# A graph and mixture-of-experts layer on Trainium2: experts add straight into the output, and ScalarE multiplies all chunks of the early edge batches

## What is computed

```python
edge_index = jnp.stack([src, dst])                    # 50000 edges, 3125 nodes, sorted by dst
xn = _layernorm(x, axis=-1)                           # x: 3125 x 256
x = x + gnn(xn, edge_index, W, att_src, att_dst, bias) + mix(xn, Wqkv, Wproj, temperature)
x = x + ffn(_layernorm(x, axis=-1), Wg, W1, W2)       # 8 experts, 2 for each token
# gnn: h = x @ W; alpha = softmax over the edges of a node of leaky_relu(a_src[src] + a_dst[dst])
#      out = segment_sum(alpha[:, :, None] * h[src], dst)
# mix: y = sum over second order (pair) features of q against sums over all nodes of k, k, v
# ffn: top-2 gate; out = sum of prob * (relu(x @ W1[e] + b1[e]) @ W2[e] + b2[e])
```

## Time and profile before

| | us |
|---|---|
| median of 3 runs | 1449.74 |
| lowest and highest | 1444.14, 1452.1 |
| the profiled execution, its own time | 1443.35 |
| its span, first to last instruction | 1441.3 |
| PE busy in the span | 1202.2 (83%) |
| DVE / ACT / POOL busy | 847.1 / 609.0 / 669.3 |
| feature steps with edges, and steps 29 to 32 | about 309 to 597 |
| mix stage | about 597 to 912 |
| stores of the attention and mix rows, issued by SP | 929.9 to 960.9 |
| first instruction that waits for these stores (DVE, the slots' one-hots) | 985.7 |
| experts | about 1013 to 1428 |

### The profile page before, as it was taken

How to read it: one execution, slowest core, us unless ns; L and a number is a source line. 1 busy time by engine, 2 the same in 40 slices (tenths; PEclk the granted TensorE clock), 3 DMA queues, 4 the chain that set the end, 5 groups by cost and what they waited for, 6 DMA issues and landing times.

```text
span 1441.3 us, 25299 instructions
## 1 busy us (share of the span) xinstructions
PE 1202.2 (83%) x7992; PEld 865.4 (60%) x7993; DVE 847.1 (59%) x1771; ACT 609.0 (42%) x1967; POOL 669.3 (46%) x626
## 2 busy tenths in 40 slices
PE   3789956748778877899999999275999999999994
PEld 2645533425444544545455556174899999999994
DVE  8599859788888887644545446878222233332221
ACT  1400011444554446587777777250333333333331
POOL 2070000675556556777777777630333333333331
PEclk9999966779988988999999999657999999999997
DMA  5635374432222223333434333773122222222223
GB/s 178 213 121 198 140 283 140 141 94 74 79 83 82 78 80 92 99 114 100 117 114 117 103 115 113 289 277 131 31 36 37 37 36 36 36 36 36 36 36 103
DMA packets 67570, 153.67 MB, mean 107 GB/s; under 512 B 12962, under 2 KB 41559, under 8 KB 66263
## 3 DMA queue, kind: packets, MB, share of 16 engines
q0 software_dynamic: 32640, 75.27, 21.0%
q1 hardware_dynamic: 33478, 74.93, 14.7%
q10 hardware_dynamic: 1360, 2.33, 0.5%
HBM read 131.76 MB, written 23.92 MB: 108 GB/s over the span
## 4 chain that ended last, share of the span: by engine, by line
PE 66%; DVE 20%; issue 4%; DMA 3%; POOL 2%; ACT 1%; DVEq 1%; SPq 0%; POOLq 0%; ACTq 0%
PE ps L1267 15%; PE ps L1560 14%; PE ps L1570 13%; DVE arena L1829 4%; PE ps L1463 4%; PE ps L1208 4%; PE ps L1475 3%; PE ps L1296 2%; PE ps L1217 1%; PE ps L1421 1%; DVEq L1833 1%; PE ps L1175 1%; POOL arena L853 1%; DVE arena L1786 1%; DMA h_d<-arena 1%
## 5 line engine op out<-in xcount | busy, mean ns | idle before, releaser
L853 POOL DMA_INDIRECT arena<-h_d,tables x440 | 449.1, 1021 | 189.5 <-issue 126.1
L1267 PE MATMUL ps<-arena 128*128 128x264 f32 x880 | 246.1, 434 | 86.2 <-DVE acc L1838 63.6
L1267 PEld LDWEIGHTS ps<-arena 128*128 128x128 f32 x880 | 181.2, 214 | 143.9 <-issue 91.4
L970 ACT ACTIVATE arena<-arena 128x64 f32<-128x64 f32 x880 | 222.0, 339 | 17.6 <-DMA arena<-h_d,tables 17.6
L1560 PE MATMUL ps<-acc 128*128 128x128 f32 x1792 | 211.3, 277 | 0.0
L895 POOL DMA_INDIRECT sum_d<-acc,tables x56 | 89.8, 1603 | 254.9 <-DVE acc L2217 247.4
L1560 PEld LDWEIGHTS ps<-acc 128*128 128x128 f32 x1792 | 206.5, 193 | 0.3
L1570 PE MATMUL ps<-arena,acc 128*128 x896 | 202.5, 379 | 0.0
L1137 ACT ACTIVATE acc<-ps,b_s 128x128 f32<-128x128 f32 x448 | 128.1, 369 | 120.1 <-PE ps L1560 120.1
L1570 PEld LDWEIGHTS ps<-arena,acc 128*128 128x128 f32 x896 | 166.0, 190 | 20.3
L2205 DVE COPY acc<-arena 128x1024 f32 x112 | 78.3, 700 | 123.8 <-PE ps L1560 123.3
(11 more groups left out here) (368 smaller groups left out, 1489.6 us busy)
## 6 DMA issues: line engine op xcount, KB each, us to landing
arena<-dl_d SPq DMA_DIRECT2D x22, 640.0 KB, 6.9
arena<-lo_d SPq DMA_DIRECT2D x16, 784.0 KB, 4.4
arena<-h_d,tables POOLq DMA_INDIRECT x440
arena<-in_w SPq DMA_DIRECT2D x4, 1664.0 KB, 11.7
arena<-in_w SPq DMA_DIRECT2D x4, 1632.0 KB, 25.5
arena<-hi_d SPq DMA_DIRECT2D x16, 343.0 KB, 5.1
h_d<-arena SPq DMA_DIRECT2D x25, 128.0 KB, 1.7
sum_d<-res SPq DMA_DIRECT2D x5, 640.0 KB, 7.9
```

Of the source, the lines that this page charges most:

```text
L853: pool.indirect_dma_start(gb[u][:, k, 0:D], None, h_d, bass.IndirectOffsetOnAxis(tsrc[:, j:j + 1], 0)).then_inc(s_gg[u], 16)
L970: ins = A_.activation(v, v, ACT.Copy, scale=wm[:, m + k, h:h + 1])
L1267: last = MM(ps[:, 6 + s, 0:ACOL], oh[b % OB][:, m, :], gb[u][:, m, :], start=(k == 0), stop=(k == TE - 1))
```

## The change

The scratch tensor `sum_d` goes. SP stores the attention and mix rows into `out`, the last tile apart (one DMA more), the experts add into `out`, with a bound on the index so that padding rows are skipped, and the last copy is gone, as is a store of zeros to `sum_d`'s padding rows. Thresholds of `s_zero` and `s_res` follow. In batches below `early` = 50, ACT multiplies all four chunks (16 instructions), DVE's multiply (1853) is left out, and the one-hot instruction raises `s_msg` in its place.

```diff
             for c in range(LC):
                 sp.wait_ge(s_att2, c + 1)
-                sp.dma_start(sum_d[c * LW * P:(c + 1) * LW * P, :].rearrange("(t p) c -> p t c", p=P),
-                             res[:, c * LW:(c + 1) * LW, :]).then_inc(s_res, 16)
+                a, b = c * LW, min((c + 1) * LW, NT - 1)
+                sp.dma_start(ot[:, a:b, :], res[:, a:b, :]).then_inc(s_res, 16)
+                if c == LC - 1:
+                    sp.dma_start(out[(NT - 1) * P:N, :], res[0:TAIL, NT - 1, :]).then_inc(s_res, 16)
...
-            sp.wait_ge(s_fy, 16 * NJ)
-            sp.dma_start(out.rearrange("n c -> (n c)").rearrange("(p w) -> p w", p=P),
-                         sum_d[0:N, :].rearrange("n c -> (n c)").rearrange("(p w) -> p w", p=P)).then_inc(s_res, 16)
             sp.wait_ge(s_res, 16 * (LC + 1))
...
-                pool.indirect_dma_start(sum_d, bass.IndirectOffsetOnAxis(pidx[:, j:j + 1], 0),
-                                        ys[j % 2], None, compute_op=ALU.add).then_inc(s_fy, 16)
+                pool.indirect_dma_start(out, bass.IndirectOffsetOnAxis(pidx[:, j:j + 1], 0),
+                                        ys[j % 2], None, bounds_check=N - 1, oob_is_err=False,
+                                        compute_op=ALU.add).then_inc(s_fy, 16)
...
-                for k in range(KA, SB * TE):
+                for k in range(0 if b < early else KA, SB * TE):
                     for h in range(GH):
                         v = gb[u][:, k, h * GD:(h + 1) * GD]
                         ins = A_.activation(v, v, ACT.Copy, scale=wm[:, m + k, h:h + 1])
...
-                    V.tensor_tensor(oh[b % OB], under(iota_f[:, :], SB * TE), over(tdl[:, m:m + SB * TE], P), ALU.is_equal)
+                    ins = V.tensor_tensor(oh[b % OB], under(iota_f[:, :], SB * TE), over(tdl[:, m:m + SB * TE], P), ALU.is_equal)
+                    if b < early:
+                        ins.then_inc(s_msg, 1)
                     if b >= 2:
                         accumulate(b - 2, 1)
-                    dve.wait_ge(s_gg[u], 16 * SB * TE * (b // NBUF + 1))
-                    v = gb[u][:, 0:KA, 0:D].rearrange("p k (h c) -> p k h c", c=GD)
-                    V.tensor_tensor(v, v, over(wm[:, m:m + KA, 0:GH], GD), ALU.mult).then_inc(s_msg, 1)
+                    if b >= early:
+                        dve.wait_ge(s_gg[u], 16 * SB * TE * (b // NBUF + 1))
+                        v = gb[u][:, 0:KA, 0:D].rearrange("p k (h c) -> p k h c", c=GD)
+                        V.tensor_tensor(v, v, over(wm[:, m:m + KA, 0:GH], GD), ALU.mult).then_inc(s_msg, 1)
```

More of the change, by code:

```diff
@@ L164, in gps_layer @@
         xn_d = dram("xn_d", [NP + P, D])
-        sum_d = dram("sum_d", [NP + P, D])
         AW = 32000
@@ L746, in _ @@
             sp.dma_start(xn_d[NP:NP + P, :], zrow).then_inc(s_zero, 16)
-            sp.dma_start(sum_d[NP:NP + P, :], zrow).then_inc(s_zero, 16)
             sp.wait_ge(s_wl, 1)
@@ L876, in _ @@
                 ins.then_inc(s_own, 1)
-            pool.wait_ge(s_zero, 32)
+            pool.wait_ge(s_zero, 16)
             pool.wait_ge(s_xst, 16 * LC)
@@ L894, in add_results @@
                 pool.wait_ge(s_fw, j + 1)
-                pool.indirect_dma_start(sum_d, bass.IndirectOffsetOnAxis(pidx[:, j:j + 1], 0),
-                                        ys[j % 2], None, compute_op=ALU.add).then_inc(s_fy, 16)
+                pool.indirect_dma_start(out, bass.IndirectOffsetOnAxis(pidx[:, j:j + 1], 0),
+                                        ys[j % 2], None, bounds_check=N - 1, oob_is_err=False,
+                                        compute_op=ALU.add).then_inc(s_fy, 16)
             for j in range(JB - 1):
                 load_tokens(j)
-            pool.wait_ge(s_res, 16 * LC)
+            pool.wait_ge(s_res, 16 * (LC + 1))
             for j in range(NJ):
@@ L1941, in bulk_weights @@
                 dve.wait_ge(s_we, 1)
-                dve.wait_ge(s_zero, 32)
+                dve.wait_ge(s_zero, 16)
                 dve.wait_ge(s_bias, NT)
@@ L2179, in _ @@
             dve.wait_ge(s_xst, 16 * LC)
-            dve.wait_ge(s_res, 16 * LC)
+            dve.wait_ge(s_res, 16 * (LC + 1))
             for k in range(TOPK):
```

## The result

| | before | after |
|---|---|---|
| median, us (20 runs each) | 1449.57 | 1443.81 |
| lowest and highest | 1443.32, 1452.10 | 1441.86, 1447.19 |
| the profiled execution, its span | 1443.35, 1441.3 | 1443.57, 1441.8 |
| last add starts (POOL) | 1424.52 | 1432.42 |
| from there to the end of the span | 16.78 | 9.38 |

The ratio of the runs is 0.997, with a 95% interval of 0.996 to 0.998. The medians lie 5.8 us apart (the ratio makes it 4.3); 13.9 were forecast (1436). Faster was right, the size was not. The profile of before came from one of its fastest executions, that of after from a median one, so the two profiles must not be subtracted as a whole: 7.9 us that after is late at the last add are partly that luck.

A forecast was written before the change was run, and what follows sets the result against it. Bounds: a PE-DVE cycle in feature steps, PE in the mix stage, the uncovered copy at the end. 1443.35 - 12.5 - 1.9 + 0.5 = 1429.5, median 6.4 higher: 1436; range 1426 to 1446.

The forecast's parts named there:

- The copy, -12.5: At the kernel's end: nothing runs beside the copy, so removing it saves 12.5 of the 12.95 us from its issue.
- it doesn't do what it says: Rival at the end: the last add might wait for something else; the prediction saw nothing; no chance listed under this name.
- The adds into `out`, 0 with bounds -2.3 and +3.2: Experts' 56 adds on POOL: a bound check is hidden by 4.4 us idle; 0, between 2.3 sooner and 3.2 later.
- DVE in the steady steps, 0: Feature steps: two DVE multiplies fewer per step only lengthen DVE's idle time by 0.6 us; saved 0.
- ACT's loop, 12.07 against 11.89: Feature steps: ACT's longer loop is hidden in long steps (13.35 us) and 0.18 us over in short ones (11.89).
- 0.5 for the whole stretch: Feature steps from 312 to 534 us: three short steps, lengthened by ACT's loop, cost 0.5 us together.
- PE come to batch 45 0.6 sooner: Before the mix stage: without DVE's multiply of batch 41, PE starts aggregating batch 45 at 589.0, not 589.61.
- The rival in which the clock turns the other way (0.1): Feature steps: three short steps turn long at the low clock, 4.4 us more, giving 1440; chance 0.1, to 1444.
- The entry of the mix stage, 3 us of waits, and the squares 3.4 later: Steps 27 to 32: PE waits for ACT 1.0 and 2.0 us, first squares start at 601.75 instead of 598.38.
- The gathers, -2.2: POOL's gathers between 562 and 598 us: six no longer stretched by DVE's multiplies, last rows land 2.2 us earlier.
- The end of the edge work, -1.9: Where gathers (904.9) meet ACT's last batch (905.2): the later decides, 905.2 for 907.09, saved 1.9 us.
- a slower add: Rival: the bound check or `out` makes adds longer; below 4.4 us each, at most 8.8, 1445; chance 0.08, to 1446.

The follow-up runs named there:

- e6: Output part and no drain, ACT multiplying all four chunks in batches 0 to 37 alone, against the kernel before: ratio 0.9939.
- e7: Output part and no drain, ACT multiplying all four chunks in batches 38 to 49 alone, against the kernel before: ratio 0.9939.
- e12: Output part and no drain, ACT multiplying all four chunks in every second batch of 38 to 49, against the kernel before: 1431.88 us, ratio 0.9909.
- e1: Output part alone (adds into `out` with bound, copy gone, batches shared as before), against the kernel before: 1440.33 us, ratio 0.9967.
- e4: The kernel before without POOL's drain, against the kernel before: 1445.90 us, ratio 0.9996.

## Why the prediction was right, and where it failed

**The copy, -12.5: this step failed. The copy's size was right, what runs beside it was not seen.** "Nothing runs beside the copy" was read from the rows; in the trace of before, 12.5 us of copy hid the 6.3 us of POOL's drain, and taking the cover away exposed it. Between the last add's start and the end 16.78 became 9.38: 7.4 saved, of which 1.1 is the earlier landing, so the copy gave 6.3. This term was 6.2 too large, three quarters of the 8.1 that the sum missed. The prediction's own criterion (the span ends within 1 us of the last add's landing) was the one that failed, and pointed at it. The rival "it doesn't do what it says" said "I see nothing": the question to ask was which engines finish beside the copy, and what each still has to do. The page of the Trainium skill that the prediction sets beside the copy ("DMA: Bandwidth & Descriptors", section "Anatomy of one DMA — SWDGE (gpsimd) path") fits DMAs issued by GpSimd, and this one was issued by SP, so its 9.3 us bear on neither side.

**The adds into `out`, 0 with bounds -2.3 and +3.2: right in sum, as two things cancel that it did not have.** The group of adds, whose answer before is the earlier trace rows:

```profile
L892 POOL DMA_INDIRECT out<-acc,tables x56 | 89.4, 1596 | 255.2 <-DVE acc L2218 247.5 <-issue 5.1 <-DMA out<-acc,tables 2.6
```

1.596 for 1.603, so the add itself costs POOL no more, and the last add, in all kernels with the bound, lands after 2.7 instead of 3.8. That padding rows without a transfer make it shorter was argued, and not measured apart.

Against this gain of 1.1 the slots of the experts run slower. From the start of the 28th add to that of the 50th it is 159.4 us in the three profiles with `sum_d` and 160.6 to 161.1 in the thirteen with adds into `out`. Three slots take 7.5 to 7.7 for 7.1 to 7.3; ahead of the first, POOL's gather of tokens takes longer (the output part alone, then the kernel before), and PE's next products start 4.03 after the ones before them, for 3.67:

```profile
1234.70 1.44 POOL L885 DMA_INDIRECT acc<-xn_d,tables  x1 [0.30 <-issue]
```

```profile
1234.53 0.99 POOL L887 DMA_INDIRECT acc<-xn_d,tables  x1 [0.30 <-issue]
```

From PE's last product of the mix stage (917.87 and 911.06) to the last add it is 514.55 in the changed kernel for 513.46: 1.1 lost. The forecast's "hidden" held for the adds and not for what POOL does between them. Which piece of the output part does it was not tested.

**DVE in the steady steps, 0: right.** No profile shows a step shortened by the missing multiplies; changing the steady batches alone (e6) gained nothing.

**ACT's loop, 12.07 against 11.89: right to 0.01.** The step of 12.08 went back to 11.9 where ACT had 1.8 to spare. What 0.5 for the whole stretch left out is how many steps are short. From the first aggregation (312.86 in the profile of before) to that of batch 45, five profiles of kernels with the old share took 276.8 (three of them, four short steps with the first, of 12.0) or 281.3 (two, one short step); of the changed share four took 283.0 to 283.2 (one short step) and one 279.5 (three). So the changed steps cost 1.8 within the pattern of one short step and 6 across patterns, and the profile of before was of the favourable kind. Of the 1.8, some 1.2 lie in the steady steps, where long ones of 13.5 to 13.6 became more frequent, and 0.65 behind them, where the forecast had PE come to batch 45 0.6 sooner: no such gain shows in the changed kernel. (With the last twelve batches alone changed, e7, this stretch is 0.4 shorter than with none, so what becomes of the 0.6 stays open.) The rival in which the clock turns the other way (0.1) comes nearest to this. The granted clock shows that the place of the low stretch moves: the first microsecond of two long steps, before and after (columns as in rows 4), one still at 2.4 GHz and one mostly at 1.2.

```profile
363.60:364.60 1.00, 1.00 (x5) 0.80 (x6) 1.00 (x3) 1.00 (x5) 0.00 (x0) 1.00 0.43 131
```

```profile
379.32:380.32 1.00, 1.00 (x3) 0.80 (x4) 0.79 (x2) 1.00 (x6) 0.12 (x1) 0.58 0.33 86
```

Where the low stretch lies in a step moves from step to step, and a step that it misses is short. What decides which execution gets four such steps and which gets one stays open.

**The entry of the mix stage, 3 us of waits, and the squares 3.4 later: right in kind (2.5 of waits; 3.3 from the aggregation to the squares, where the forecast had 4.0 less the 0.6 above).** And e12 shows it to be ACT's lead that is lost, since half as many extra multiplies there bring no wait.

**The gathers, -2.2: right in kind.** Between 562 and 600 us the gathers took 2.8 more than 0.945 each before, and 1.0 after. (The forecast's 2.24 passed over two stretched gathers, at 575.27 and 597.14.) POOL's waits for PE there grew by 1.0, since PE came later. The Trainium skill ("SBUF — State Buffer", section "SBUF: two separate sides") would have DVE's multiply lock POOL out for a whole instruction. The runs agree that DVE and POOL get in each other's way, but not with that size: nine multiplies of 0.69 gone gave 1.8 back, not 6.

**The end of the edge work, -1.9: this step failed.** It took ACT's idle time before its last batch (4.29) for the slack of the whole stream. But the mix stage is PE's, and PE waited only 2.11 for that batch. A stream that enters 3.3 late and can give back some 2.1 ends 1.2 late, not 1.9 early: 3 us, on the other side of nought. From the first squares to PE's last product of the stage it was 911.06 - 598.38 = 312.7 before and 917.87 - 607.79 = 310.1 after (312.5 and 310.1 in the kernels with none and all 50, side by side), so 2.5 came back for 3.3 paid. That is not one number either: with the changed share the stage took 310.1 in all five profiles, with the old one 311.3 to 315.9 in five, and PE's wait for the last batch 0.7 to 3.7. Together with the steps that makes +2.6 for the batches' part, against a measured +1.3 (by the ratio +1.9, 0 to 3.9) alone and +4.1 side by side.

The sum as it should have read: -7.4 at the end, +1.1 in the experts, +0.8 for entry and end of the edge work, +1.8 in the steps: -3.7, on the median of before. The measured medians differ by 5.8, the ratio by 4.3. Of the rivals none had the drain; that the range, 1426 to 1446, held the time was luck: its upper end was there for a slower add and for the clock, and the main cause was neither. The forecast's own range, 1429 to 1442, did not.

## What to carry to other kernels

Before a last transfer is taken away, list for every engine what it still has to finish at that time: the gain is the distance to the next thing that ends, and an instruction that the profile leaves out (here a drain) can be that thing; a stretch without any row at the end of the span is how it looks. The slack that counts at a meeting of two streams is the idle time on the engine that carries the path behind it, not that of the engine that feeds it. Moving work to an engine that runs ahead costs its lead exactly where the lead was needed; giving it half the work (every second batch of the last twelve) kept the lead. Whether that is also faster than moving nothing (2.3 us by the medians) is not shown.

## What the runs showed of the hardware that was not expected

POOL's drain at the end of this program, which has indirect DMAs, took 6.3 us (9.38 against 3.12 from the last add to the end), with no row in the views, no DMA traffic and PE's granted clock at 0.50 in it. It starts when POOL reaches it, also while an add is in flight (8.04). What it guards, and whether a program may do without it, no run here shows. The Trainium skill ("VectorE: DVE Perf Modes", section "The DRAIN you can't avoid") tells of the runtime's own drains around a kernel, which take 12 ns on all five engines. This one is put in by the program's block, and its 6270 ns are 500 times that; SP's drain at the same place took 7 ns.

The time of a loop whose PE part meets the two levels of the clock is not a constant of the program: the same program (output part, no drain, no batch changed) took 276.8 us from the first aggregation to that of batch 45 in one profile and 281.3 in another, on another chip. That it is not the chip alone is seen in the first group: on one chip, with the old share, 276.8 (e1) and 281.3 (e4). Compared across the two kinds, a change worth 1.8 there looks like one worth 6.3.
